# Collecting expert results rank by rank inside the expert loop, with two transfers moved, in a Perceiver-style block

## The reference, cut to what matters

```python
tidx, tw = _gate(x)              # 8 of 64 experts for each token
def body(acc, ws):               # over the 64 experts
    wg, wu, wdn, cw = ws
    hmid = silu(x @ wg) * (x @ wu)
    return acc + cw[:, None] * (hmid @ wdn), None
return y + shared_expert(x)
```

## Time and profile before

| | us |
|---|---|
| median of three runs (921.66 to 929.37) | 927.86 |
| profiled execution, own time | 924.3 |
| its span | 922.5 |
| PE busy | 690.4 (75%) |
| DVE busy | 447.2 (48%) |
| POOL busy | 249.8 (27%) |
| ACT busy | 243.6 (26%) |

### The profile page before, as it was taken

The page is one execution under the profiler, slowest core; times in us unless marked ns, Lnnn a source line. Parts: engine busy times, 40 slices in busy tenths (PEclk is TensorE's granted clock), DMA queues, the critical chain, the costliest instruction groups (busy, mean ns, idle before and its releaser), DMA issues. The chain is left out here.

```text
span 922.5 us, 18970 instructions
## 1 busy us (share of the span) xinstructions
PE 690.4 (75%) x6637; PEld 473.8 (51%) x6637; DVE 447.2 (48%) x1114; ACT 243.6 (26%) x471; POOL 249.8 (27%) x289
## 2 busy tenths in 40 slices
PE   6798389896867699998899979796649899990000
PEld 4355155644645355555654468685448777770000
DVE  4333023357756452232436649858834334437534
ACT  1122021166445121211223644203412223330000
POOL 1011000020134120000000436512235445526775
PEclk9899699988968599999979965579779999995555
DMA  8999999420028969999117942001049999972343
GB/s 344 380 402 330 355 404 410 159 91 1 2 58 316 322 246 334 405 411 392 72 35 163 213 114 74 4 2 47 1 132 334 331 304 300 310 259 88 116 115 105
DMA packets 70888, 195.62 MB, mean 212 GB/s; under 512 B 11832, under 2 KB 43552, under 8 KB 65824
## 3 DMA queue, kind: packets, MB, share of 16 engines
q1 hardware_dynamic: 41248, 155.31, 47.6%
q10 hardware_dynamic: 22752, 20.72, 6.8%
q0 software_dynamic: 6816, 18.62, 6.8%
HBM read 181.05 MB, written 21.95 MB: 220 GB/s over the span
## 5 line engine op out<-in xcount | busy, mean ns | idle before, releaser
L2086 POOL DMA_INDIRECT moe_xg<-xn_rows,moe_idx x78 | 73.9, 948 | 83.4 <-DVE moe_idx L2029 72.3
L2128 POOL DMA_INDIRECT moe_yg<-y_rows,moe_sloti x64 | 64.0, 1000 | 37.2 <-issue 19.2
L302 PE MATMUL ps<-x0ctxT,x0qcur 128*64 128x512 f32 (+1 forms) x256 | 51.9, 562 | 22.8 <-DMA x0ctxT<-ctx_T 18.4
L1472 POOL TENSOR_TENSOR ss_dec<-ss_dec,ss_cT 128x256 f32<-128x256 f32 x48 | 39.7, 860 | 91.4 <-ACT ss_dec L1427 51.3
L2045 DVE TENSOR_TENSOR moe_hidT<-moe_silu,ps 128x128 f32<-128x128 f32 (+1 forms) x64 | 20.3, 317 | 80.5 <-ACT moe_silu L2062 59.6
L1285 PE MATMUL ps<-xnT,w_win 128*128 128x512 f32 x128 | 59.0, 620 | 0.0
L327 PE MATMUL ps<-x0ctxN,x0pT 128*64 128x256 f32 (+1 forms) x416 | 46.6, 381 | 7.4 <-issue 5.2
L327 PE MATMUL ps<-x1ctxN,x1pT 128*64 128x256 f32 (+1 forms) x416 | 46.6, 380 | 7.4 <-issue 5.2
L1317 PE MATMUL ps<-ss_dec 64*64 64x32 f32 (+2 forms) x1792 | 46.1, 256 | 6.1 <-issue 4.5
L91 POOL TENSOR_TENSOR rstd<-vare,neghalf 128x2 f32<-128x2 f32 (+1 forms) x10 | 11.2, 1125 | 139.5 <-DVE vare L87 139.5
L2062 ACT ACTIVATE moe_silu<-ps 128x128 f32<-128x128 f32 (+1 forms) x64 | 19.2, 300 | 109.0 <-issue 72.2
(11 more groups left out here) (387 smaller groups left out, 1384.6 us busy)
## 6 DMA issues: line engine op xcount, KB each, us to landing
x0ctxT<-ctx_T SPq DMA_DIRECT2D x8, 3202.0 KB, 25.4
x1ctxT<-ctx_T SPq DMA_DIRECT2D x8, 3202.0 KB, 13.6
x0ctxN<-ctx SPq DMA_DIRECT2D x8, 3072.0 KB
x1ctxN<-ctx SPq DMA_DIRECT2D x8, 3072.0 KB
y_rows<-moe_ysb ACTq DMA_DIRECT2D x78, 128.0 KB
moe_gate_up_weights<-moe_gate_up SPq DMA_DIRECT2D x36, 256.0 KB, 4.5
e_shared_gate_up_weights<-moe_gate_up SPq DMA_DIRECT2D x28, 256.0 KB, 4.9
ss_dec<-seg_rows SPq DMA_DIRECT2D x8, 768.0 KB, 17.0
```

What stands on the lines that cost most here:

```text
L302: mm = pe.matmul(ps[64 * b:64 * b + 64, n, 0:k1 - k0], qcur[:, u, h, 64 * b:64 * b + 64], ctxT[:, u, b, h, k0:k1], start=h == 0, stop=h == ...
L1472: e.tensor_tensor(f, f, g, ALU.mult).then_inc(s, 1)
L2086: nc.gpsimd.indirect_dma_start(out=xg[:, m, :], out_offset=None, in_=xn_rows, in_offset=bass.IndirectOffsetOnAxis(ap=idx[:, m:m + 1], axis ...
L2128: nc.gpsimd.indirect_dma_start(out=yg[:, j, k * D:(k + 1) * D], out_offset=None, in_=y_rows[0:MOST_TILES * P, :], in_offset=bass.IndirectO ...
```

## The change

There are three parts.

1. **Rank by rank.** The third Block is gone. After its last gather of rows for the tiles, POOL goes through ranks k = 7 down to 0. For each it loads `needed[k]` into a register (the number of rounds after which all slots of that rank are stored), waits until each of the six ring places has been stored that many times, and issues 8 gathers. DVE computes `w8` right after its part of the loop and adds rank by rank, with a drain for every 8 adds. `needed` is worked out in the choice Block: a maximum over tokens on DVE, a transpose and a small product on PE, and five small operations on DVE. `yg` has its own memory beside the rings.
2. **Spare rows** are filled from SP's stream in the latent attention's Block, behind the feed-forward's weights.
3. **First ten weight sets.** Six whole and four shared sets (gate, up and down) are loaded by SP in the choice Block once `etab` is copied. The expert loop loads none of them. `LEAST` goes from 2 to 3 and `LEAST2` from 1 to 2 as bounds of the counts; two rounds stay written out (`WRITTEN`).

```diff
@@ latent attention, SP
                         issue(sp, WF.loads)
+                        for r in range(SPARE):
+                            t0, t1 = T * 8 // P + r * NT, ...
+                            sp.dma_start(y_rows[t0 * P:t1 * P, :], a["x"]...).then_inc(s_spare, 16)
@@ experts' choice, SP
                     sp.dma_start(xn_rows..., xn[:]).then_inc(s_rows, 16)
+                    sp.wait_ge(s_eb, 1)
+                    def load_first(x, n, gate_up, loaded, down, down_loaded):
+                        e = sp.value_load(etab[0:1, x, n:n + 1], min_val=0, max_val=E - 1)
+                        sp.dma_start(gate_up[:, n]..., a["moe_gate_up"][ds(e, 1), :, :]...).then_inc(loaded[n], 16)
+                        sp.dma_start(down[:, n, :], a["L1_ffn_We_down"][ds(e, 1), :, :]...).then_inc(down_loaded[n], 16)
+                    for n in range(RING):
+                        load_first(0, n, wgu, s_wl, wdn, s_wd)
+                    for n in range(4):
+                        load_first(1, n, wgu2, s_wl2, wdn2, s_wd2)
@@ experts' choice, PE
+                    pe.wait_ge(s_lt, 1)
+                    pe.transpose(ps[0:8, 2, 0:P], latest[:], ident[:]).then_inc(s_lr, 1)
                     for j in range(NT):
+                        if j == 4:
+                            pe.wait_ge(s_lt, 2)
+                            pe.matmul(ps[0:1, 2, P:P + 8], latest_row[:, 0:1], ident[0:8, 0:8], ...).then_inc(s_lr, 1)
@@ experts' choice, DVE
+                    nc.vector.tensor_reduce(latest[:], slots8[:].rearrange("p j k -> p k j"), AX, ALU.max).then_inc(s_lt, 1)
                     for j in range(NT):
+                        if j == 2:
+                            dve.wait_ge(s_lr, 1)
+                            nc.vector.tensor_reduce(latest_row[:], ps[0:8, 2, 0:P], AX, ALU.max).then_inc(s_lt, 1)
...
+                    dve.wait_ge(s_lr, 2)
+                    nc.vector.tensor_scalar(latest_int[:], ps[0:1, 2, P:P + 8], -1.0, None, ALU.add)
...
+                    nc.vector.tensor_scalar(needed[:], latest_int[:], 1, None, ALU.add)
                     dve.wait_ge(s_im, NT)
@@ expert loop, DVE, behind its steps: choice_weights(), 24 weight_third(i), then
+                    for k in reversed(range(8)):
+                        if k:
+                            dve.wait_ge(s_yg[k], 16 * NT)
+                        for j in range(NT):
+                            if k == 0:
+                                dve.wait_ge(s_yl[j], 16)
+                            ins = nc.vector.scalar_tensor_tensor(xt[:, j, :], yg[:, k, j, :], w8[:, j, k:k + 1], xt[:, j, :], ALU.mult, ALU.add)
...
+                        dve.drain()
@@ expert loop, ACT
                         if live(0):
+                            if isinstance(n, int) and n < RING or isinstance(q, int):
+                                pass
@@ expert loop, POOL
+                    def collect(k):
+                        rounds = pool.value_load(needed[0:1, k:k + 1], min_val=1, max_val=MOST + MOST2)
+                        stored = nc.gpsimd.to_reg(rounds * 16)
+                        pool.wait_ge(s_rows, 16)
+                        for m in range(RING):
+                            pool.wait_ge(s_ys[m], stored)
+                        for j in range(NT):
+                            nc.gpsimd.indirect_dma_start(out=yg[:, k, j, :], ..., in_=y_rows[0:MOST_TILES * P, :],
+                                                         in_offset=...(ap=sloti[:, 0, j, k:k + 1], axis=0)
+                                                         ).then_inc(s_yg[k] if k else s_yl[j], 16)
                     run(pool, step, 0)
+                    for k in reversed(range(8)):
+                        collect(k)
@@ expert loop, SP
-                    for g in range(LEAST):
+                    for g in range(1, WRITTEN):
                         whole(g)
...
-                    shared(0, None)
@@ x0
-            for r in range(SPARE):
-                ...
-                sp.dma_start(y_rows[t0 * P:t1 * P, :], ...).then_inc(s_spare, 16)
```

More of the change, by code:

```diff
@@ L1654, in experts @@
             w8 = own("w8", [P, NT, 8])
+            yg = own("yg", [P, 8, NT, D])
+            latest = own("latest", [P, 8])
+            latest_row = own("latest_of_choice", [8, 1])
+            latest_int = own("latest_int", [1, 8], I32)
+            needed = own("rounds_needed", [1, 8], I32)
             pick = own("pick", [P, NT, E])
@@ L1765, in _ @@
                             act.wait_ge(s_et, 1)
[L1766 removed]
+                            nc.scalar.copy(etab[:].rearrange("o x t -> o (x t)"), ps[0:1, 3, 0:2 * P]).then_inc(s_eb, 1)
                         act.wait_ge(s_mk, j + 1)
@@ L1942, in run @@
             def run(eng, step, lag):
-                for n in range(LEAST * RING):
+                for n in range(WRITTEN * RING):
                     step(n, n % RING, n // RING, None, lambda k, n=n: n >= k)
@@ L1953, in shared @@
                         step(g * RING + m, m, g, q, lambda k: True)
-                with eng.Fori(LEAST, first) as g:
+                with eng.Fori(WRITTEN, first) as g:
                     whole(g)
@@ L2049, in _ @@
                     run(dve, step, GU)
[L2050 to L2077, removed]
-                    act.wait_ge(s_spare, SPARE * 16)
-                    run(act, step, DOWN + 1)
@@ L2080, in _ @@
-                @block.gpsimd
-                def _(pool):
-                    def step(n, m, g, q, live):
-                        ready = nc.gpsimd.to_reg(n + 1)
-                        pool.wait_ge(s_rows, 16)
-                        pool.wait_ge(s_ic, ready)
-                        nc.gpsimd.indirect_dma_start(out=xg[:, m, :], out_offset=None, in_=xn_rows,
-                                                     in_offset=bass.IndirectOffsetOnAxis(ap=idx[:, m:m + 1], axis=0)
-                                                     ).then_inc(s_ga[m], 16)
-                    run(pool, step, 0)
-                    rounds = whole_rounds(pool) + shared_rounds(pool)
-                    for m in range(RING):
-                        pool.wait_ge(s_ys[m], rounds * 16)
@@ new lines, in _, with load, whole, shared @@
+                @block.sync
+                def _(sp):
+                    def load(n, expert, dst, signal):
+                        e = sp.value_load(expert, min_val=0, max_val=E - 1)
+                        wait(sp, s_gu, n - RING + 1)
+                        sp.dma_start(dst.rearrange("p h f -> p (h f)"),
+                                     a["moe_gate_up"][ds(e, 1), :, :].rearrange("o p f -> p (o f)")).then_inc(signal, 16)
+                    def whole(g):
+                        for m in range(RING):
+                            load(g * RING + m, etab[0:1, 0, ds(g * RING + m, 1)], wgu[:, m], s_wl[m])
+                    def shared(q, g):
+                        for m in (0, 2, 3, 5):
+                            x = shared_set(m)
+                            load(g * RING + m, etab[0:1, 1, ds(q * 4 + x, 1)], wgu2[:, x], s_wl2[x])
+                    for g in range(1, WRITTEN):
+                        whole(g)
+                    first = whole_rounds(sp)
+                    second = shared_rounds(sp)
+                    with sp.Fori(WRITTEN, first) as g:
+                        whole(g)
+                    with sp.Fori(1, second) as q:
+                        shared(q, first + q)
@@ L2174, in experts @@
+            rings.close()
             st.close()
```

149 lines of the change are left out of this document (81 added, 68 removed).

## The result

The changed kernel took 886.42 us (median of 885.66 to 891.11), the kernel before 924.76 beside it: ratio 0.963, 95% interval 0.954 to 0.972. The forecast was 889 with 878 to 903. The profiled execution took 887.0, its span is 885.2.

What follows compares the result with a forecast made beforehand. At the end POOL's issuing of gathers was taken as the bound, in x0 spare copies holding the DMA engines. Terms -23.8 - 0.7 - 12.1 = -36.6 took 924.3 to 887.7; with a run-spread allowance 889 us, range 878 to 903.

Steps and rivals of the forecast that it cites:

- the DMA's pace of x1: x0 from step 4: full DMA engines set the pace, 80.7 us to the last product as in x1; 23.8 us gained.
- the term's upper end: x0 from step 4: PE's own pace, 14.64 us a step without waits, sets the time; up to 27 us gained.
- Rival A: x0: only the pause of 16.6 us is given back, DMA paces the rest as now; 895 us, chance 0.12.
- Rival D: x0's steps 4 to 7 and after: without its pause PE loses clock; slower, 959 us, chance 0.02.
- Rival E: Latent stage: the copies hold up its code or x1's loads, at most 28 us; 917 us, chance 0.05.
- Barrier: Choice Block's end: all engines meet there and SP's loads make it late, +1.0 us (0 to 3).
- `needed` +0.5: Choice Block: computing `needed` adds work ahead of or between that of PE and DVE, +0.5 us (0 to 1).
- First gathers: Expert loop's start: first gathers no longer share the queues with the weights, -2.2 us (0 to -3.5).
- start of collection: POOL after its tile gathers: first collecting gather at about 816.5 in place of 834.25, -17.7 us.
- number loads and waits: POOL's queue in the collection: each rank's number load, multiplication and waits cost 0.7 us, +5.6 us for eight.
- Rival C: Collection: POOL's gathers all take 1419 ns, 27 us more in 64; 915 us, chance 0.04.
- Rival B: Collection: ranks come late because the waits ask for all rounds, POOL starts at 834; 905 us, chance 0.04.

Runs made afterwards that it cites:

- changed_again: The changed kernel itself, measured once more with nothing altered, as base for the follow-up kernels: 883.0 us, ratio 0.957 to the kernel before.
- changed_third: The changed kernel itself, measured a third time with nothing altered: 880.6 us, ratio 0.952 to the kernel before.
- adds_after_all: The changed kernel, but DVE waits for all 64 collecting gathers before its first add: 907.1 us, ratio 0.978 to the kernel before.

## Why the prediction was right

**Part 1** (-23.8 forecast). Measured -25.2 in A, and 23 and 26 us by undoing and by doing it alone. The mechanism, copies in front of the columns, was right. The pace that I took for what follows was not: I had taken the DMA's pace of x1, and in the trace after steps 4 to 7 run at PE's, 14.55 us a step, with one wait over 1 us, of 1.60. That was the term's upper end, so little hung on it. In changed_again the last two steps take 14.8 and 16.3 us, and the gain in A is 23.1. Rival A, that only the pause is given back, is refuted: the steps behind it went from 16.4 to 14.5. Rival D failed too: the scores of steps 4 to 7 took 5.60 us each, the length that they have in x1 at clock 1.00. Rival E: the copies have landed by about 199 us (the last is issued at 171.9, the slowest takes 27.5), SP issues its next load at 245.0, and the first scores of x1 start 143.3 us behind the last product of x0 in both traces. B doesn't grow either (487.7 before, 479 to 491 with the copies there, 484.1 with them in x0), though its spread alone would hide some us. The 917 of this rival counts from 889, where the others count from 887.7; on their base it is 916.

**Part 2** (-0.7). Measured +0.5 from `etab` to the first silu, inside its bounds, though with the other sign; in the other traces of the changed kernel it was +0.4 and 0. Barrier +1.0: the measured +2.2 was in the bounds (0 to 3); the number of issues was right, but a set took 1.60 us, not 1.54, and DVE left only when SP's last issue was over. `needed` +0.5: from `etab` to the list of rows it is 15.0 us in the trace after and 15.0 to 15.4 in those of the experiments, 14.8 before: 0.2 to 0.6. First gathers -2.2: the fourth tile is turned 3.0 us behind its gather instead of 5.0, and from entry to silu 2.0 us are gained.

**Part 3** (-12.1). From the first silu to the end -14.8. Its terms: start of collection relative to the last tile gather -17.4 (forecast -17.7); number loads and waits +5.6 forecast and at most 0.3 measured, the one term that failed: seven ranks start after the usual 0.30, only rank 7 after 0.60 (which the start's -17.4 contains). The price of a number load was right (0.68 in the open), the place was not. I had taken every instruction in POOL's stream as a gap in its work, though gathers of 0.95 us stand in front of it. In this trace part of what it should have cost was lost elsewhere: gathers longer by 3.9 us and 0.4 in the tail. In changed_again and changed_third it is 17.0 and 17.4 us less from the first silu to the end, so there the missing 5.6 us show nearly whole. The tile loop was 1.7 us shorter; at C's spread I claim nothing from that.

Rival C was right in kind and wrong in size: 0.7 to 3.9 us over three traces, not 27. The Trainium skill says, in SBUF — State Buffer, section "Who interferes with whom", that a DVE instruction with two SBUF inputs contends with a GpSimd instruction that reads SBUF. The adds read `moe_yg` and `xt`, and the traces agree in part: most gathers that start within a burst take 1.03 to 1.68 us in place of 0.95, but 4 of 18 in the trace after stay at 0.95. Whether it is that port that holds them up no run here shows; adds_after_all shows only that it is DVE's work. Rival B is refuted by the first collecting gather, 1.55 us behind the last tile gather; in wait_all_rounds, where every rank waits for all rounds, it comes 16.0 us later than that.

**The sum** (-36.6 forecast) is -37.3 between the two profiled executions: the missing number loads (-5.6), 1.4 more in part 1 and a loop shorter by 1.7 stand against 3.9 for gathers, 1.2 more for the barrier, 2.2 us in B, whose spread is larger than that, and 0.7 of small ones. So the closeness of 889 to 886.4 is partly luck: errors of 5.6 and 3.9 us stood against each other in this trace, and the median of the changed kernel itself moved between 880.6 and 886.4.

## What to carry to other kernels

Fill memory that nobody reads soon from the stage whose DMA slices are empty, and check the place by the pace of the same loop without that traffic. An order of collection that follows the data's order of completion is worth about the barrier wait that it removes (here 17.4 us), provided the waits ask for what each part needs; one round too early, and here the waiting queue starved the loop that it overlaps for 3.33 us. Extra instructions on a queue are priced by where they stand: behind work that the engine still has to do they were free, behind a wait they cost their full length.

## What the hardware showed that I had not expected

- The stretch from x0's last product to `etab` took 479 to 491 us in the twelve profiled executions of the table, whatever was changed. A gain of a few us can be claimed only from a milestone near the change.
- A number load on POOL: 0.68 us for each of three more ahead of rank 7, where the gathers before it had waited for indices; 0 ahead of the seven ranks whose gathers before had not.
- DVE's adds, and its computation of the weights before them, lengthen indirect gathers on POOL from 0.95 us to 1.29 in a burst of adds (1.68 in one trace) and to 1.46 beside the weights. Gathers beside neither took at most 0.95.
- The copies from memory to memory cost SP more in the new place, 6.40 us for eight issues against 5.05: one issue took 1.98 us, and in every trace with the copies there one takes 1.9 to 2.5. The slowest copy landed 27.5 us after its issue against 23.5. The only loads near them are the weights ahead; the cause stays open.
